# Pyramid-pooled attention in fp32 on one core: the last batch convolved in two rounds, exp and probabilities in PSUM

## What is computed

```python
qk  = relu(bn(conv1x1(x, qk_w)))            # 256 channels
val = relu(bn(conv1x1(x, v_w)))             # 512 channels
key, value = psp(qk), psp(val)              # adaptive max pools to 1, 9, 36 and 64 cells: 110 cells
scores = softmax(query . key * 256**-0.5)   # query is qk, 4096 positions by 110 cells
y = scores . value                          # 512 channels
out = x + bn(conv1x1(y, out_w))
```

## Time and profile before

| what | us |
|---|---|
| median of 3 runs | 1428.84 (1428.83 to 1429.14) |
| the profiled execution | 1426.75 |
| its span | 1424.9 |
| TensorE busy | 1387.3 |
| VectorE busy | 917.8 |
| ScalarE busy | 474.8 |
| GpSimd busy | 240.2 |
| TensorE in the chain that ended last | 95% of the span |

### The profile page before, as it was taken

How to read it: one execution, slowest core, us unless ns; L and a number is a source line. 1 busy time by engine, 2 the same in 40 slices (tenths; PEclk the granted TensorE clock), 3 DMA queues, 4 the chain that set the end, 5 groups by cost and what they waited for, 6 DMA issues and landing times.

```text
span 1424.9 us, 15729 instructions
## 1 busy us (share of the span) xinstructions
PE 1387.3 (97%) x6029; PEld 1134.4 (80%) x6029; DVE 917.8 (64%) x1745; ACT 474.8 (33%) x662; POOL 240.2 (17%) x141
## 2 busy tenths in 40 slices
PE   7999999999999999999999999999999999999776
PEld 6888888888888888888888888888888888888654
DVE  6555656657656666657656767656766657656678
ACT  4112333333333333333333333333333332333243
POOL 0000121121121121121121121221121221221252
PEclk9999999999999999999999999999999999999989
DMA  5112234534434534434434534434524434434456
GB/s 192 60 59 90 88 118 148 178 120 146 171 125 148 177 112 155 173 122 148 162 132 150 177 119 148 167 128 148 177 106 161 169 127 148 156 132 156 142 196 223
DMA packets 102941, 204.98 MB, mean 144 GB/s; under 512 B 3243, under 2 KB 3283, under 8 KB 102867
## 3 DMA queue, kind: packets, MB, share of 16 engines
q1 hardware_dynamic: 102290, 202.93, 40.5%
q10 hardware_dynamic: 576, 1.05, 0.2%
HBM read 136.86 MB, written 67.11 MB: 143 GB/s over the span
## 4 chain that ended last, share of the span: by engine, by line
PE 95%; DVE 3%; issue 1%; ACT 1%; DMA 0%; SPq 0%
PE conv_ps L330 25%; PE conv_ps L328 25%; PE conv_ps L329 24%; PE out_ps L367 4%; PE out_ps L368 4%; PE out_ps L369 4%; PE score_ps L342 2%; PE score_ps L343 2%; PE score_ps L344 2%; PE sum_ps L354 1%; PE sum_ps L353 1%; PE sum_ps L379 0%; PE sum_ps L381 0%; PE sum_ps L380 0%; DVE e_l L696 0%
## 5 line engine op out<-in xcount | busy, mean ns | idle before, releaser
L328 PE MATMUL conv_ps<-xh,wh 128*128 128x512 f32 x1536 | 602.2, 392 | 0.0
L330 PE MATMUL conv_ps<-xl,wh 128*128 128x512 f32 x1536 | 601.6, 392 | 0.0
L329 PE MATMUL conv_ps<-xh,wl 128*128 128x512 f32 x1536 | 598.5, 390 | 0.0
L623 DVE TENSOR_REDUCE row_max<-conv_ps 128x64 f32<-128x512 f32 (+2 forms) x576 | 289.1, 530 | 441.5 <-ACT q L471 370.8
L330 PEld LDWEIGHTS conv_ps<-xl,wh 128*128 128x128 f32 x1536 | 288.6, 188 | 63.9
L329 PEld LDWEIGHTS conv_ps<-xh,wl 128*128 128x128 f32 x1536 | 288.9, 188 | 63.2
L328 PEld LDWEIGHTS conv_ps<-xh,wh 128*128 128x128 f32 x1536 | 288.8, 188 | 61.3
L273 POOL TENSOR_TENSOR e_l<-e,e_h 128x512 fp32r<-128x512 f32 x64 | 83.5, 1305 | 1024.7 <-ACT e_h L485 1024.7
L482 ACT ACTIVATE e<-score_ps 128x512 f32<-128x512 f32 x60 | 35.8, 597 | 488.7 <-PE score_ps L344 488.7
L471 ACT ACTIVATE q<-conv_ps,shift 128x512 f32<-128x512 f32 x128 | 88.2, 689 | 305.0 <-PE conv_ps L330 305.0
L277 POOL TENSOR_TENSOR q_l<-q,q_h 128x1024 fp32r<-128x1024 f32 x64 | 157.9, 2466 | 141.8 <-ACT q_h L477 141.7
(11 more groups left out here) (117 smaller groups left out, 907.7 us busy)
## 6 DMA issues: line engine op xcount, KB each, us to landing
xa<-x SPq DMA_DIRECT2D x65, 1024.0 KB, 7.5
xo<-x SPq DMA_DIRECT2D x58, 1024.0 KB, 5.2
out<-xo SPq DMA_DIRECT2D x58, 1024.0 KB, 4.2
q<-x SPq DMA_DIRECT2D x4, 1024.0 KB, 5.3
out<-q SPq DMA_DIRECT2D x3, 1024.0 KB, 8.7
out<-xa SPq DMA_DIRECT2D x2, 1024.0 KB, 4.2
q<-v_w ACTq DMA_DIRECT2D x4, 256.0 KB, 4.3
xa<-x SPq DMA_DIRECT2D x2, 512.0 KB, 5.6
```

The source lines that it names most:

```text
L328: nc.tensor.matmul(bank(s, c)[:, :], wh[:, k, cols], hi, start=(k == 0), stop=False)
L329: nc.tensor.matmul(bank(s, c)[:, :], wl[:, k, cols], hi, start=False, stop=False)
L330: last = nc.tensor.matmul(bank(s, c)[:, :], wh[:, k, cols], lo, start=False, stop=(k == KC - 1))
L623: last = nc.vector.tensor_reduce(row_max[:, c, n, :], src[:, r0_ * W:r1_ * W].rearrange("p (r w) -> p w r", w=W), AX.X, ALU.max)
```

## The change

- **Two rounds.** Tiles 56 to 63 (the last batch) are convolved for channels 4 and 5 alone in steps 56 to 63, beside the attention of batch 6. Steps 64 to 71 (X = 72) load, split and convolve the same tiles again for channels 0 to 3. The scores and exp of the last batch (`ac` = 56 to 63) stand in steps 64 to 71; what of them is kept until the end are `e_h` and `e_l` of the probabilities. The eight projections of the last batch come last. From step 56 on, three banks serve the convolution, the fourth is a second score bank (from tile 48), and the projection uses four banks only for the last batch.
- **Keys and values apart.** `finish_grids` pools the key channels after step 63; in step 71 each value channel gets its cells, grid and value as soon as its rows are pooled, and `project_values` is issued by channel. The last vo is made in four pieces of 128 columns.
- **PSUM in place.** exp is written back to the score bank, `normalise` multiplies there, and both low parts of it are taken from there; `refine` writes its intermediate into the bank of sums. `e` and `s_r0` are gone; `e_h` and `e_l` have six slots each, the last two tiles use a slot of `q_h` and `q_l`.
- **split_e_lo** is on VectorE, GpSimd has only `split_q_lo`. The low part of x stays on VectorE.
- `scores(a)` waits for `p_lo` of the tile before in its bank instead of `exp_done`; `sums(a)` waits for `rsum_ready` instead of `s_r0_made`.

The diff, cut to its core:

```diff
+        def tile_at(s):
+            return s if s < S else s - NT
+
+        def channels(s):
+
+            return range(CC) if s < LAST else range(VC, CC) if s < S else range(VC)
+
+        def group(s, c):
+
+            if s < LAST:
+                return CC * s + c
+            if s < S:
+                return CC * LAST + QC * (s - LAST) + c - VC
+            return CC * LAST + QC * NT + VC * (s - S) + c
+
+        GROUPS = CC * S
         def bank(s, c):
-            return conv_ps[(CC * s + c) % 4]
-
+            g = group(s, c)
+            return conv_ps[g % 4] if s < LAST else conv_ps[(g - CC * LAST) % 3]
         def score_bank(a):
-            return conv_ps[0] if a >= LAST and a % 2 else score_ps
+            return conv_ps[3] if a >= LAST - NT and a % 2 else score_ps
         def pv_bank(k):
-            return conv_ps[1] if k == B - 1 else sum_ps
+            return out_ps[1] if k == B - 1 else sum_ps
         def out_bank(a, m):
-            return [*out_ps, conv_ps[2], conv_ps[3]][m] if a >= LAST - 1 else out_ps[m % 2]
+            return [out_ps[0], *conv_ps[0:3]][m] if a >= LAST else out_ps[m % 2]
+
+        def q_slot(a):
+
+            return a % 2 if a < LAST + 2 else 0
+
+        def e_slot(a):
+
+            if a < S - 2:
+                return e_h[:, a % 6, :], e_l[:, a % 6, :]
+            qq = [q_h, q_l][a - (S - 2)]
+            return qq[:, 1, 0, :], qq[:, 1, 1, :]
         def residual(a):
             if a < LAST:
                 return xo[:, a % 2, :, :]
             q2 = [q[:, 2 * i:2 * i + 2, :, :].rearrange("p t c n -> p (t c) n") for i in range(4)]
-            return [xa[:, 0, :, :], xa[:, 1, :, :], q2[0], q2[1], xo[:, 0, :, :], xo[:, 1, :, :], q2[2], q2[3]][a - LAST]
+            return [xo[:, 0, :, :], xo[:, 1, :, :], q2[0], q2[1], q2[2], xa[:, 0, :, :], q2[3], xa[:, 1, :, :]][a - LAST]
...
-            for s in range(S):
-                if s >= NT:
-                    if s >= NT + 2:
-                        stored(s - NT - 2)
-                    load_residual(s - NT)
-                if s + 2 < S:
+            for s in range(X):
+                if s < LAST:
+                    if s >= NT:
+                        if s >= NT + 2:
+                            stored(s - NT - 2)
+                        load_residual(s - NT)
                     sp.wait_ge(x_lo, 2 * s + 2)
                     load(s + 2)
-                if s == S - 2:
-                    sp.wait_ge(x_lo, 2 * (S - 2) + 2)
-                    load_residual(LAST)
-                if s == S - 1:
-                    sp.wait_ge(x_lo, 2 * S)
-                    load_residual(LAST + 1)
-                if s >= NT + 1:
-                    store(s - NT - 1)
-
...
+                    if s >= NT + 1:
+                        store(s - NT - 1)
+                    continue
+                if s + 2 < X:
+                    sp.wait_ge(x_lo, 2 * s + 2)
+                    load(s + 2)
+                if s - NT - 2 < LAST:
+                    if s > LAST:
+                        store(s - NT - 2)
+                    stored(s - NT - 2)
+                    load_residual(s - NT)
+
+                if s in (S + 1, S + 3, S + 5, S + 7):
+                    a = LAST + [2, 3, 4, 6][(s - S) // 2]
+                    sp.wait_ge(q_lo, LAST + s - S + 1)
+                    load_residual(a)
+                if s == X - 1:
+                    sp.wait_ge(x_lo, 2 * X - 2)
+                    load_residual(LAST + 5)
+                    sp.wait_ge(x_lo, 2 * X)
+                    load_residual(LAST + 7)
+            for a in range(LAST, S - 1):
...
-            def split_e_lo(a):
-                pool.wait_ge(e_hi, a + 1)
-                wait(pool, out_done, OC * (a - 2))
-                u = a % 3
-                nc.gpsimd.tensor_tensor(e_l[:, u, :], e[:, u, :], e_h[:, u, :], ALU.subtract).then_inc(e_lo, 1)
-
             def split_q_lo(a):
                 pool.wait_ge(q_hi, a + 1)
-                nc.gpsimd.tensor_tensor(q_l[:, a % 2, :, :], q[:, a % NT, :, :], q_h[:, a % 2, :, :], ALU.subtract)\
+                u = q_slot(a)
+                nc.gpsimd.tensor_tensor(q_l[:, u, :, :], q[:, a % NT, :, :], q_h[:, u, :, :], ALU.subtract)\
                     .then_inc(q_lo, 1)
-            for s in range(S):
-                if s >= NT:
-                    split_e_lo(s - NT)
-                if s >= NT - 1:
-                    split_q_lo(s - (NT - 1))
...
+            for a in range(S):
+                split_q_lo(a)
...
             def conv(s, c):
-                wait(pe, rows_pooled, CC * s + c - 3)
+                g = group(s, c)
+                wait(pe, rows_pooled, g - 3 if g < CC * LAST + 3 else g - 2)
                 for k in range(KC):
-                    if c == 0 and k % HALF == 0:
+                    if c == channels(s)[0] and k % HALF == 0:
...
-                wait(pe, exp_done, a - 1 if a > LAST else a)
-                if a == LAST + 1:
-                    pe.wait_ge(rows_pooled, CC * S)
-                sc, u = score_bank(a)[0:ROWS, :], a % 2
+
+                wait(pe, p_lo, a - 1 if a > LAST - NT else a)
+                if a == LAST - NT + 1:
+                    pe.wait_ge(rows_pooled, CC * LAST)
+                sc, u = score_bank(a), q_slot(a)
...
-                wait(pe, s_r0_made, a)
+                wait(pe, rsum_ready, a)
...
+                if a == LAST:
+                    pe.wait_ge(vo_lo, B + m)
+                    wait(pe, rows_pooled, GROUPS)
+                elif m == 0 and a % NT == 0:
+                    pe.wait_ge(vo_lo, a // NT + 1)
+                wait(pe, out_added, OC * a + m - (3 if a > LAST else 1))
...
+            def project_values(k, m):
+                if k < B - 1:
+                    pe.wait_ge(value_ready, k + 1)
+                    wait(pe, rsum_ready, NT * k)
                 else:
-                    wait(pe, out_added, OC * a + m - (3 if a >= LAST else 1))
...
+                    pe.wait_ge(value_ready, B + m)
...
+            for s in range(LAST, S):
+                ap, ac = s - NT - 1, s - NT
+                sums(ap)
+                if s == LAST:
+
+                    conv(s, 4)
+                scores(ac)
+                if s > LAST + 1:
+                    project(ap - 1, 2)
+                    project(ap - 1, 3)
+                if s > LAST:
+                    conv(s, 4)
+                conv(s, 5)
+                project(ap, 0)
+                project(ap, 1)
+                if s == LAST:
+                    for m in range(VC):
+                        project_values(ac // NT, m)
+                    project(ap, 2)
+                    project(ap, 3)
+            for s in range(S, X):
+                ap, ac = s - NT - 1, s - NT
+                sums(ap)
+                if s == S:
+                    project(ap - 1, 2)
+                    project(ap - 1, 3)
+                conv(s, 0)
+                conv(s, 1)
+                if s == S:
+                    project(ap, 0)
+                    project(ap, 1)
+                scores(ac)
+                conv(s, 2)
+                if s == S:
+                    project(ap, 2)
+                    project(ap, 3)
+                conv(s, 3)
+            for m in range(VC - 1):
+                project_values(B - 1, m)
...
+            sums(S - 1)
+            project_values(B - 1, VC - 1)
...
-                wait(act, p_lo, a - 2)
-                nc.scalar.activation(e[:, a % 3, :], score_bank(a)[0:ROWS, :], ACT.Exp).then_inc(exp_done, 1)
+                sc = score_bank(a)
+                nc.scalar.activation(sc[:, :], sc[:, :], ACT.Exp).then_inc(exp_done, 1)
                 act.wait_ge(exp_done, a + 1)
-                wait(act, out_done, OC * (a - 2))
-                nc.scalar.activation(e_h[:, a % 3, :], e[:, a % 3, :], ACT.Copy).then_inc(e_hi, 1)
+                if a < S - 2:
+                    wait(act, out_done, OC * (a - 5))
+                nc.scalar.activation(e_slot(a)[0], sc[:, :], ACT.Copy).then_inc(e_hi, 1)
...
+            for s in range(X):
                 ap, ac = s - NT - 1, s - NT
...
                 if ap >= 0:
                     guess(ap)
-                if s + 1 < S:
+                if LAST < s < S:
+                    exps(ac)
+                if s + 1 < X:
                     split_hi(s + 1, 0)
                 if ap >= 0:
                     split_p_hi(ap)
-                if s + 1 < S:
+                if s + 1 < X:
                     split_hi(s + 1, 1)
-                if ac >= 0:
+                if ac >= 0 and not LAST < s < S:
                     exps(ac)
-                if ac + 1 >= 0:
+                if 0 <= ac + 1 < S:
                     split_q_hi(ac + 1)
-                store_q(s, 0)
-                if ac >= 0 and ac % NT == 0:
-                    values_hi(ac // NT)
-                store_q(s, 1)
...
+                if s < S:
+                    store_q(s, 0)
```

(106 more changed lines are left out.)

236 lines of the change are left out of this document (84 added, 152 removed).

## The result

| | before | changed |
|---|---|---|
| median, us (7 runs each) | 1428.84 | 1424.46 |
| lowest to highest, us | 1426.68 to 1429.27 | 1423.20 to 1425.28 |
| profiled execution, us | 1426.75 | 1423.58 |
| its span, us | 1424.9 | 1421.9 |
| matmuls | 6029 | 6029 |

The ratio is **0.9972**, 95% interval 0.9961 to 0.9983: faster by 0.28%, 4.4 us between the medians. 6.9 us had been forecast.

A forecast was written before the change was run, and what follows sets the result against it. TensorE, busy 97% of the span, was taken as the bound: of 38.6 us to win, 31.7 are lost (7.5 in step 56, some 12 in 57 to 63, 3 in 64, 9 at the end). 1428.84 minus 6.9 gives 1421.9 us, range 1409 to 1432.

The forecast's parts named there:

- Body: Tiles 8 to 55: e_l moves to VectorE under existing cover, so nothing is lost; 29 us at stake without it.
- Step 56: Scores of tile 48 wait 5.5 us for key_l, then half clock costs 2.0; the step ends at 1193.0.
- Steps 57 to 63: VectorE bound; the second split_lo waits for GpSimd's q_l, so the mean step is 11.7 us, not 10.1.
- In-place PSUM: Refine's two operations and normalise, working in PSUM: extra cost taken as 0, upper bound 0.53 us each.
- Rival (c): In-place PSUM is dear: steps 57 to 63 each 1.6 us longer, 11 us in all, 1433; chance 0.14.
- Steps 64 to 71: TensorE bound: the first ends at 1293.1, including 1.0 for a clock dip, then seven steps of 12.8 us.
- First projection at T0 + 6.9: Tail: the last batch's projections start 6.9 us after the last convolution ends, forecast at 1382.8; channel 3's value comes at 4.8.
- Projections to the end of the matmuls, 24.0 us: Tail: 96 matmuls take 22.0 us plus 2.0 for half clock; VectorE's additions and last softmax, 21.9, just fit.
- Last store, 3.1 + 0.5 after the last addition: End of the tail: 3.1 us from the last addition to the end, plus 0.5 for nearly full store queues.
- (a): Rival, steps 57 to 63: q_l misses the second split_lo, steps take 10.1 to 10.4 us, 1411; chance 0.22.
- (b): Rival, steps 57 to 63: GpSimd's q_l starts before the first split_lo, 1.0 us more a step, 1430; chance 0.14.
- (d): Rival, slower tail: 40 us after the last convolution instead of 35.2, half clock held longer, 1427; chance 0.08.

The follow-up runs named there:

- the run without backlog: The changed kernel with the stores of tiles 57 to 60 left out: 1423.45 us, ratio 0.9971 against the kernel before.
- the second experiment: The changed kernel with both split_lo put directly behind p_lo, ahead of the addition and cells: 1432.53 us, ratio 1.0032 against the kernel before.

## Why the prediction was right, and where it was off

The direction, the cause and the place of each loss up to the last convolution were as forecast, and the tail was forecast too short; the gain was 2.5 us smaller by the medians, 3.9 by the profiled spans (1418.0 forecast, 1421.9 found).

**Body: nothing.** Right: the window from 300 to 600 us still holds 1312 matmuls, as in the earlier trace rows, and key_l of step 56 is there at 1181.92, 0.5 us from the forecast.

**Step 56.** 5.38 us of stall and half clock behind it, 5.5 and 2.0 forecast, and refine of step 57 at 1196.12 (1195.1 forecast):

```profile
1181.97 0.79 PE L351 MATMUL score_ps<-q_h,key_h 128*128 128x512 f32 x1 [5.38 <-DVE key_l L711]
1182.56 0.63 PE L352 MATMUL score_ps<-q_h,key_l 128*128 128x512 f32 x1
```

**Steps 57 to 63.** The mechanism is the forecast's best part. The first split_lo starts 2.99 us after normalise (3.01 forecast) and 0.31 ahead of GpSimd (0.34). Steps are 11.34 and 11.61 us (11.55 and 11.8 forecast), and refine of step 64 starts at 1276.00 (1276.3). That last agreement is partly luck: refine of step 57 came 1.0 us late, and the seven steps took 79.9 us where 81.2 were forecast. Taking GpSimd's operation away returned 9.6 us, which shows the cause.

**In-place PSUM.** Taken at nothing, and it is nothing. The groups of the page and of VectorE:

```profile
L726 DVE SCALAR_TENSOR_TENSOR sum_ps<-sum_ps,r 128x512 f32<-128x512 f32 x64 | 44.6, 697 | 26.9 <-ACT r L536 26.9
...
L736 DVE TENSOR_TENSOR score_ps<-score_ps,rsum 128x512 f32<-128x512 f32 x56 | 39.2, 699 | 1.9
```

0.70 us each, and behind normalise the next operation starts 0.60 us later, as it does behind the additions. Rival (c) falls. The 120 against 58 cycles of the Trainium skill (VectorE: DVE Perf Modes, "The TRN2 errata") don't show: 0.70 us stand against the 0.69 of the same operation in SBUF.

**Steps 64 to 71.** No gap in 90 us at full clock. The dip in step 64, put at 1.0, did not come in this execution, and came in others at 1.6. The last convolution ended at 1381.75, 1.0 ahead of the forecast, most of it the dip's.

**The tail is the step that failed, in three terms.** Timeline of TensorE:

```profile
1387.12 0.79 PE L388 MATMUL out_ps<-woT_h,value_h 128*128 128x512 f32 x1 [1.99 <-DVE value_l L720]
...
1389.87 0.77 PE L377 MATMUL out_ps<-e_h,vo_h 128*128 128x512 f32 x1 [1.10 <-issue]
...
1398.25 0.47 PE L377 MATMUL out_ps<-e_h,vo_h 128*128 128x512 f32 x1 [0.81 <-DVE xo L756]
```

- *First projection at T0 + 6.9*: it came at T0 + 8.1. Channel 3's value was ready at T0 + 5.3 instead of 4.8, and its product, which follows a wait of 1.99 us, ran at half clock: 1.7 us from its start to vo, where 0.7 to 1.3 had been taken. Half clock had been allowed for behind this point and not at it. It doesn't always come: behind the same wait of 1.98 to 1.99 us the product ran at full clock in four of the nine profiles with the new order, and the first projection began 2.1 to 2.2 us after the product's start instead of 2.75 (1387.12 to 1389.87). So 0.5 us of this term is the value's lateness, and 0.7 the clock of this execution.
- *Projections to the end of the matmuls, 24.0 us*: 25.1. "Just fit" was no fit: while the last softmax's operations stand among VectorE's additions, a bank comes back 0.8 us late at 1398.25.
- *Last store, 3.1 + 0.5 after the last addition*: **6.1**, the largest miss, 2.5 us. The last addition is the end of this row of VectorE's, 1415.81:

```profile
1413.76 2.05 DVE L756 TENSOR_TENSOR xa<-conv_ps,xa 128x512 f32<-128x512 f32 x3
```

The 3.1 of the earlier trace rows belong to a tail in which TensorE, stalled and at lower clock, set a slow pace for the stores. The forecast saw that 383 GB/s would be needed and priced a full queue at 0.5, instead of following the bytes: the store of tile 62 is issued whole when its additions end, at 1413.12, and the next tile's are done 2.7 us later, so 2 MB leave in one burst. SyncE's issues, then two windows (columns as in the earlier trace rows):

```profile
1413.12 0.37 SPq L228 DMA_DIRECT2D out<-q  x1
1413.87 4.39 SPq L274 DMA_DIRECT2D out<-xa  x4
```

```profile
1414.00:1416.00 2.00, 1.08 (x5) 0.56 (x3) 1.81 (x3) 0.00 (x0) 0.00 (x0) 1.00 1.04 381
1416.00:1417.00 1.00, 0.00 (x0) 0.00 (x0) 0.00 (x0) 0.00 (x0) 0.00 (x0) 1.00 1.00 360
```

At 380 GB/s 2 MB take 5.5 us, until 1418.6 at the earliest, with the rest of tile 61's store ahead of them, and behind them what a store needs beyond its bytes (in the run without backlog data flowed until just after 1420 and the span ended at 1421.4). Stores by quarter got 1.8 us of it back.

Sum: -1.0 (T0) + 1.2 + 1.1 + 0.2 (last addition) + 2.5 = +4.0, the 3.9 found.

**Rivals.** (a), engines clear of each other, was priced at 10.9 us below the forecast; it is 9.6 without the collision (K) and 7.5 with it covered, but it needs the other order. (b), GpSimd first, did not happen in any of the seven steps (the first split_lo leads by 0.30 us or more in each), and no run tests it. The run with both split_lo side by side shows what VectorE standing uncovered through GpSimd's turn is worth: 9.0 us (K), twice the whole gain, and 0.9 a step where (b) had 1.0. (d) is partly what happened: 1421.9 - 1381.75 = 40.2 us from T0 to the end, the 40 it named instead of 35.2. Its reason was mostly the drain, and the clock only in part.

The rule of the Trainium skill (SBUF — State Buffer, "Who interferes with whom"), that the instruction issued first holds the port for its whole length, agrees with the rows shown here; who is next when one waits is told by the second experiment alone.

## What to carry to other kernels

When two engines exclude each other, ask at each collision what the waiting engine could do meanwhile: put operations that don't collide there, in the length of the other's (here 2.6 us), and don't put two colliding ones side by side. When a change makes the last stretch faster, follow the last bytes out: the tail of the old kernel says nothing of a queue that had slack then. And where an intermediate is moved into a PSUM bank, ask how long the bank is then held: that cost 7.5 us in the old order, while the operation itself cost nothing.

## What the runs showed of the hardware that had not been expected

- A GpSimd operation that waits for VectorE's gets its turn between two of VectorE's that stand back to back: 4.59 us for the pair instead of 2.35. The one row of before that showed such a meeting could not tell it.
- A wait of 2.4 us at the same point of the program is followed by half clock in some executions (2.39 and 2.41 us, 1.6 us lost) and not in others (2.39 and 2.42 us, nothing lost); a wait of 1.99 us in the tail likewise (0.6 to 0.7 us). What decides it stays open; it limits what a single profile of this kernel can tell to about 2 us.
- 1 MB stores back to back leave at 360 to 393 GB/s, also when nothing had been stored for 8 us before.
